# Relational sums of a graph layer: counts matrices replaced by gathered edge rows

## The chip, the cores and the metric

The kernel runs on one core of a Trainium2 chip, in one launch. The metric is the device time of the program in microseconds. The kernel before was timed three times: 2770.32 us in the median, 2766.78 to 2781.82. A profile was taken of one further execution, whose span from the first to the last instruction is 2772.8 us.

## The reference

There are 625 nodes with 1024 features and 10,625 edges, each with a source, a destination, a weight and one of 8 types. Two layers follow each other. Layer 0 has a graph convolution, linear attention and a mixture of 16 experts. Layer 1, cut to what matters:

```
xn  = layernorm(x)
u   = xn @ root + bias
for r in range(8):                         # the edge types, "relations"
    sums = segment_sum(xn[src] * (type == r), dst)     # 625 x 1024
    cnt  = segment_sum((type == r), dst)
    u    = u + (sums / max(cnt, 1)) @ weight[r]        # weight[r] is 1024 x 1024
z   = concat(u, xn) @ w_gate + b_gate
gnn = tanh(u) * z + xn * (1 - z)
mix = linear_attention(xn) @ Wout + bout               # 16 heads, needs Wqkv first
x   = x + gnn + mix
x   = x + small mixture of experts(layernorm(x))
```

All of it is in float32. The kernel gets float32 products out of TensorE's fp32r mode by splitting each operand into a high and a low part and adding three products (high by high, low by high, high by low).

## The kernel before

The 625 nodes are 5 blocks (T) of 125 (TP). The transposed normalized input lies in SBUF as T_h and T_l. A weight matrix of 1024 x 1024 comes in 8 chunks of 128 x 1024 (512 KB): SyncE loads chunk after chunk into three raw buffers (wr), ScalarE makes the high part (`a_high`, line 709), VectorE the low part (`v_low`, line 224), into two pairs ws0 and ws1. `t_nat` multiplies one half (512 columns) of such a matrix: 4 chunks, 10 steps each, 3 matmuls with 512 columns in every step, into 5 PSUM banks, one for each node block. 3 of the 8 banks are then free for other work.

Every engine runs one list of instructions in a fixed order. There is no planner. What is put between the steps of a product is written by slots: `blocks()` gives each chunk of 10 steps its first slot, and `t_nat(..., slot=)` calls `t_tally` after every step.

Layer 1 in the kernel before, in order:

1. `t_attention`: Wqkv products, feature maps, attention sums (24 chunks of Wqkv). ScalarE's table for exp is loaded once in it.
2. The window: root (8 chunks), Wout (8) and the product of relation 0 (8), 240 steps. Into them go 123 tallies. `t_tally` multiplies a one-hot of sources (blc, made by GpSimd, line 2220) with a step function of targets (bod, one ScalarE Sign activation of 128 x 628, line 2169), 2 matmuls of 314 columns in bf16. VectorE adds the two halves into an int16 accumulator (acc, line 220), and SyncE stores it to DRAM. Their differences along the nodes are, for each relation, the 625 x 625 matrix of edge counts (A).
3. `t_relations`: for each relation the product y_r = xn @ weight[r] (80 steps, 240 matmuls), ScalarE and VectorE take it out of PSUM as high and low parts (nat_h, nat_l), `t_count_in` sums the counts of each node (25 matmuls of 8 columns), and `t_sums` multiplies the counts matrix with y_r: 2 halves, 5 x 5 blocks, 2 parts, so 100 matmuls of 512 columns. VectorE scales them by 1/count and adds them to u (ua, line 220).
4. `t_gate`: xn and u times w_gate, 160 steps. u is transposed during the first 40 of them (line 2794); tanh, the difference with the kept xn (xnk) and the gate sums follow.

Ahead of that, in layer 0, the edges are sorted twice on VectorE and scattered to DRAM by GpSimd: by blocks of sources for the convolution, and into 40 buckets (8 relations by 5 blocks) for the tallies (`v_sort`). The convolution itself already works by one-hots: 96 pieces of 128 edges in 32 groups of 3, a group belonging to one node block.

Of the kernel before, what the change touches and what calls it, by code (L numbers as in the profile page):

```python
# [3 lines left out]
ALU = mybir.AluOpType  # L4
# [13 lines left out]
EC = 85  # L18
NCH, NBK = 123, 40
NG, GC = 32, 3  # L20
NW = NG * GC
TALLY0 = 18
# [217 lines left out]
class Program:  # L240
    def __init__(self, nc, a, out):
# [5 lines left out]
        self.d_edges = nc.dram_tensor("scr_edges", (128 * NCH, 4), F32).ap()  # L247
        self.d_adj = nc.dram_tensor("scr_adj", ((NBK + 1 + NCH) * 128, NT), I16).ap()
# [13 lines left out]
        self.tallied_at = {TALLY0 + 5 * c // 3: c for c in range(NCH)}  # L262
        self.regs = [nc.alloc_register(mybir.EngineType.DVE, f"adj{i}") for i in range(8)]
        self.slots = [nc.alloc_register(mybir.EngineType.SP, f"slot{i}") for i in range(4)]
# [3 lines left out]
    def memory(self, nc):  # L268
# [51 lines left out]
        pair("A", R3 + 15168, 3140)  # L320
# [12 lines left out]
        at("soh", U, NBK * EC, BF16)  # L333
        at("ssc", U + 6816, NBK * EC, BF16)
        at("st1", U + 13632, NBK // 2 * EC)

        for i in range(7):
            at(f"acc{i}", R3 + 20224 + i * 1280, NT, I16)
        for i in range(7):
            at(f"bod{i}", R3 + 30336 + i * 1280, NT, BF16)  # L340
        for i in range(4):
            at(f"blc{i}", R3 + 39296 + i * 256, 128, BF16)

        for i in range(2):
            at(f"steps{i}", R3 + i * 6304, T * NT, I16)
        at("brow_u", R1, 1024)
# [67 lines left out]
        small("oneb", 128, BF16)  # L414
        spair("om", 512)
        B = o[0]
        small("et1", 1280)
        at("seb", B, NCH * 4)
        at("bias", B + 1984, NCH)
        at("same", B + 2496, NCH + 1)  # L420
        at("brows", B + 3008, NCH, I32)
        at("bslot", B + 3520, NCH)
        at("bod7", B + 3520, NT, BF16)
        at("blc4", B + 4800, 128, BF16)
        at("row", B, 1024)
        at("rwp", B, 1024, F32R)
        at("none", B, NCH * 4)
# [3 lines left out]
        at("n32", B + 2880, NBK, I32)  # L431
        at("widx", B + 3040, EC, I32)
        at("dg", B + 3392, NCH + 1, F32R)
        at("idx", B + 4000, EC, I32)
# [4 lines left out]
        small("bkr", NCH + 1)  # L439
# [14 lines left out]
        small("shift", T)  # L454
        for n in ("lg", "pr", "o1", "o2", "q1"):
            small(n, T * 16)
# [25 lines left out]
    def weights(self):  # L482
# [54 lines left out]
        qkv = lambda c: W.add(("qkv", c), a["Wqkv"][c], 1024, 2, pool=c == 8)  # L537
# [11 lines left out]
        for r in range(8):  # L549
            for h in range(2):  # L550
                for i in range(4):
                    W.add(("rel", r, h, i), W2(a["rel"][r], 2 * i, 2 * i + 2, h), 1024, 2)
# [45 lines left out]
    def tensor(self, e):  # L598
        q = Line(e, self.counting)
        self.t_features(q)  # L600
        self.t_mix0(q)
        self.t_adjacency(q)
        self.t_spread(q)
        self.t_layernorm(q, 1)
        self.t_experts(q)
        self.t_layernorm(q, 2)
        self.t_attention(q)
        self.t_relations(q)
        self.t_gate(q)
        self.t_layernorm(q, 3)  # L610
        self.t_ffn(q)

    def scalar(self, e):
# [8 lines left out]
        self.a_high(q, ("qkv", 8))  # L622
        self.a_layernorm(q, 2)
        self.a_attention(q)
        self.a_relations(q)
# [4 lines left out]
    def vector(self, e):  # L630
# [8 lines left out]
        self.v_layernorm(q, 2)  # L639
        self.v_attention(q)  # L640
        self.v_relations(q)
# [4 lines left out]
    def gpsimd(self, e):  # L646
# [4 lines left out]
        self.p_low(q, ("qkv", 8))  # L651
        self.p_keep(q)
        self.p_tallies(q)
        self.p_relations(q)
        self.p_gate(q)

    def sync(self, e):
        q = Line(e, self.counting)
        a, m = self.a, self.m
        blocks = self.blocks()  # L660
# [6 lines left out]
        for c in self.W.all:  # L667
# [6 lines left out]
            n = self.W.of[c.key] - self.W.of["root", 0, 0] - 4  # L674
            if 0 <= n < 24:
                self.s_store_tallies(q, self.tallies(blocks[n][2]))
# [35 lines left out]
    def a_place(self, q, c):  # L712
# [5 lines left out]
        elif c.key == ("w1", 0):  # L718
            q.wait_ge(self.s("aggregated"), ("sum", 7, 1, T - 1))
# [37 lines left out]

    def t_first(self, q, key, L):

        outs = self.t_pair(q, key)  # L760
        hi, lo = self.t_chunk(q, key)
        for i, t in ((0, 2), (1, T - 1)):
            q.wait_ge(*self.ps.done(("ln", L, t), 1, "low"))
            for k in range(KD):
                c = slice(k * 128, (k + 1) * 128)
                ins = mm3(q.e, outs[i:i + 1], (hi[:, c], lo[:, c]), self.Tk(k)[i:i + 1], k == 0, k == KD - 1)
        ins.then_inc(*self.s("product").up(key))
# [24 lines left out]
    def t_nat(self, q, name, h, nk, lhs, ready=None, more=(), slot=None, last=None):  # L792
# [8 lines left out]
        for i in range((nk + 1) // 2):  # L801
# [6 lines left out]
            for at, (j, t) in enumerate(steps):  # L808
                k = 2 * i + j
                if ready:  # L810
                    q.wait_ge(*ready(k))
# [9 lines left out]
                if slot is not None:  # L821
                    self.t_tally(q, slot + 10 * i + at)
# [68 lines left out]

    def t_chunk_ends(self, q):
        e, m, ps = q.e, self.m, self.ps
        b, = ps.take("chunks", 1)
        for emptied in ps.before("chunks"):
            q.wait_ge(*emptied)
        q.wait_ge(self.landed("cst_all"), 0)
        q.wait_ge(self.s("sorted"), "chunk ends")
        mm(e, ps.one(b, 128, 0, NCH + 1), m["ones"][0:NCH, :], m["dg"][0:NCH, :], True, True).then_inc(*self.s("sort_sums").up("chunks"))
# [38 lines left out]
    def v_features(self, q):  # L938
# [32 lines left out]
        end, base = self.v_ends(q, "weighted", T, 1, 128 * GC, "wssc")  # L971
# [13 lines left out]
        off, at = m["off"][0:1, :], m["o2"][0:1, 0:NG]  # L985
        ts(e, at, self.iota[0:1, 0:NG], end[0:1, 0:1], None, ALU.is_ge).then_inc(*S.up())
        for b in range(1, T - 1):
# [2074 lines left out]
```

## Time and profile before

| | us |
|---|---|
| median of 3 runs | 2770.32 |
| profiled execution, span | 2772.8 |
| PE (matmul) busy | 2662.3, 96% |
| PEld (weight load) busy | 2167.4, 78% |
| DVE busy | 1726.8, 62% |
| ACT busy | 1289.3, 46% |
| POOL busy | 530.7, 19% |
| DMA mean | 165 GB/s, 458.31 MB |

PE is TensorE, PEld its weight loads, DVE VectorE, ACT ScalarE, POOL GpSimd, SP SyncE. Matmuls are pipelined and overlap in the record, so PE's busy share says that it always had something under way, and its rate is to be read from the starts of matmuls that follow each other. The profiled execution's own device time is not shown beside its span; the span lies 2.5 us above the median of the three runs.

### The profile page before, as it was taken

To read this page: it belongs to the slowest core of one execution; us is meant where nothing else is said; L and a number is where in the kernel's file an instruction comes from. 1 tells how busy PE (TensorE), PEld (TensorE's weight loads), DVE (VectorE), ACT (ScalarE), POOL (GpSimd) and SP (SyncE) were. 2 spreads that over 40 slices of the span, in tenths; PEclk is the share of its full clock that TensorE was granted. 3 is DMA by queue.
4 is the path that set the end of the run, shared out by engine and by line. 5 is a ranking of instruction groups with operands and counts; after the bars stand their busy time and mean duration, and the time that the engine had idled before them with its cause. 6 is when DMAs were issued, how large, how long until landed. Compare 5 with 4: busy or idle time off the path is not lost.

```text
span 2772.8 us, 35121 instructions
## 1 busy us (share of the span) xinstructions
PE 2662.3 (96%) x13835; PEld 2167.4 (78%) x13835; DVE 1726.8 (62%) x2061; ACT 1289.3 (46%) x1667; POOL 530.7 (19%) x502
## 2 busy tenths in 40 slices
PE   7999999999999999999989998999999999999999
PEld 6978788777777767666889997666788888878788
DVE  7579556788777887888655656886333233335353
ACT  4337225666667666777356656664111112212121
POOL 5869025223210000000200001443200000002100
PEclk9999999999999999999999999999999999999999
DMA  5342057999999999999621111555211122121212
GB/s 165 82 128 64 31 158 254 330 328 330 329 320 333 323 328 335 338 336 334 201 76 47 39 42 52 159 158 163 92 65 65 53 73 72 61 83 46 84 58 76
DMA packets 163198, 458.31 MB, mean 165 GB/s; under 512 B 26233, under 2 KB 54777, under 8 KB 163034
## 3 DMA queue, kind: packets, MB, share of 16 engines
q1 hardware_dynamic: 128122, 409.11, 42.4%
q0 software_dynamic: 20416, 33.77, 4.8%
q10 hardware_dynamic: 14496, 13.17, 1.5%
q8 instruction: 111, 1.82, 0.3%
q14 instruction: 53, 0.43, 0.1%
HBM read 412.13 MB, written 43.65 MB: 164 GB/s over the span
## 4 chain that ended last, share of the span: by engine, by line
PE 78%; DVE 9%; DMA 7%; ACT 3%; issue 2%; POOL 1%; SPq 0%; DVEq 0%; ACTq 0%; POOLq 0%
PE ps L199 77%; DMA er<-in_wd 3%; DVE es_l L224 2%; ACT es_h L709 2%; DMA er<-in_wg 1%; DVE od L216 1%; DVE Aw L212 1%; DMA scr_ei<-xn,sdi 1%; DMA wk<-in_Wk 1%; PE ps L1906 1%; DMA yg<-scr_eo,sgi 0%; POOL scr_ei L2099 0%; DVE T_l L224 0%; DVE x L212 0%; DVE ws_l L224 0%
## 5 line engine op out<-in xcount | busy, mean ns | idle before, releaser
L224 DVE TENSOR_TENSOR es_l<-er,es_h 128x1408 fp32r<-128x1408 f32 (+1 forms) x455 | 653.7, 1445 | 185.2 <-ACT es_h L709 181.8
L709 ACT ACTIVATE es_h<-er 128x1408 fp32r<-128x1408 f32 (+1 forms) x455 | 563.4, 1242 | 250.4 <-PE ps L199 166.4
L709 ACT ACTIVATE ws_h<-wr 128x1024 fp32r<-128x1024 f32 (+1 forms) x169 | 178.0, 1055 | 644.3 <-PE ps L199 635.1
L224 DVE TENSOR_TENSOR ws_l<-wr,ws_h 128x1024 fp32r<-128x1024 f32 x167 | 207.2, 1241 | 327.5 <-ACT ws_h L709 327.2
L199 PE MATMUL ps<-ws_h,T_h 128*125 128x512 f32 x880 | 355.9, 404 | 0.0
L199 PE MATMUL ps<-ws_l,T_h 128*125 128x512 f32 x880 | 347.4, 395 | 0.0
L199 PE MATMUL ps<-ws_h,T_l 128*125 128x512 f32 x880 | 347.3, 395 | 0.0
L199 PE MATMUL ps<-es_h,xe_h 128*98 128x512 f32 (+1 forms) x768 | 208.0, 379 | 11.5 <-DVE es_l L224 11.3
L199 PE MATMUL ps<-es_h,xe_l 128*98 128x512 f32 (+1 forms) x768 | 204.6, 374 | 0.0
L199 PE MATMUL ps<-es_l,xe_h 128*98 128x512 f32 (+1 forms) x768 | 204.6, 374 | 0.0
L199 PEld LDWEIGHTS ps<-ws_h,T_l 128*125 128x125 f32 x880 | 163.2, 185 | 41.7
L199 PEld LDWEIGHTS ps<-ws_h,T_h 128*125 128x125 f32 x880 | 163.5, 186 | 40.7 <-DVE ws_l L224 0.3
L199 PEld LDWEIGHTS ps<-ws_l,T_h 128*125 128x125 f32 x880 | 163.0, 185 | 37.6
L199 PEld LDWEIGHTS ps<-es_h,xe_h 128*98 128x98 f32 x768 | 119.2, 163 | 59.1 <-DVE es_l L224 19.9
L199 PEld LDWEIGHTS ps<-es_l,xe_h 128*98 128x98 f32 x768 | 125.0, 163 | 38.1
L199 PEld LDWEIGHTS ps<-es_h,xe_l 128*98 128x98 f32 x768 | 125.0, 163 | 38.1
L199 PE MATMUL ps<-T_h,ws_h 128*128 128x314 f32 x656 | 152.1, 309 | 1.0 <-DVE ws_l L224 0.7
L199 PE MATMUL ps<-T_l,ws_h 128*128 128x314 f32 x656 | 150.1, 307 | 0.0
L199 PE MATMUL ps<-T_h,ws_l 128*128 128x314 f32 x640 | 145.9, 307 | 0.0
L220 DVE SCALAR_TENSOR_TENSOR acc<-acc,same,ps 128x314 int16<-128x314 int16 x244 | 120.8, 537 | 35.3 <-PE ps L199 30.9
L220 DVE SCALAR_TENSOR_TENSOR ua<-ps,m,ua 125x512 f32<-125x512 f32 x80 | 60.0, 751 | 120.9 <-PE ps L199 120.9
L2169 ACT ACTIVATE bod<-cst,bias 128x628 bf16<-128x628 f32 x123 | 100.1, 818 | 70.9 <-PE ps L199 69.4
(455 smaller groups left out, 5271.4 us busy)
## 6 DMA issues: line engine op xcount, KB each, us to landing
er<-in_wg SPq DMA_DIRECT2D x128, 704.0 KB, 6.6
er<-in_wu SPq DMA_DIRECT2D x128, 704.0 KB, 5.9
er<-in_wd SPq DMA_DIRECT2D x176, 512.0 KB, 5.1
wr<-in_rel SPq DMA_DIRECT2D x64, 512.0 KB, 3.6
scr_adj<-acc SPq DMA_DIRECT2D x123, 157.0 KB, 2.4
wr<-in_Wqkv SPq DMA_DIRECT2D x24, 512.0 KB, 3.5
wr<-in_gate SPq DMA_DIRECT2D x16, 512.0 KB, 3.6
wr<-in_w SPq DMA_DIRECT2D x13, 512.0 KB, 3.6
```

The source lines that it names most:

```text
L199: return e.matmul(out, l, r, start=start, stop=stop, skip_group_check=True)
L212: return e.tensor_tensor(out, x, y, op)
L216: return e.tensor_scalar(out, x, s1, s2, op0) if op1 is None else e.tensor_scalar(out, x, s1, s2, op0, op1)
L220: return e.scalar_tensor_tensor(out=out, in0=x, scalar=s, in1=y, op0=op0, op1=op1)
L224: return e.tensor_tensor(lo, src, hi.bitcast(F32), ALU.subtract)
L709: q.e.activation(c.hi, c.at, ACT.Copy).then_inc(*self.s("high").up(c.key))
L1906: ins = q.e.transpose(ps.one(bs[f // 4], 128, (f % 4) * C0, C0), self.m["eh"][0:C0, f * 128:(f + 1) * 128], self.ident[0:C0, 0:C0])
L2169: q.e.activation(self.m[f"bod{c % 8}"], self.iota, ACT.Sign, bias=self.m["bias"][:, c:c + 1]).then_inc(*self.s("chunk_signs").up(c))
```

## The change

The edges are now sorted into 5 buckets by the block of the destination, in pieces of 128 edges, three pieces to a group, 96 pieces in 32 groups. `t_relations` moves ahead of `t_attention`. It makes y_r for all 8 relations, ScalarE alone takes them out of PSUM in float32, and SyncE stores them to DRAM (scr_y, 5000 rows of 4 KB). Once, after relation 1, `t_counts` makes edge counts by node and relation with 96 matmuls of 8 columns; VectorE turns them into 1/count, and GpSimd gathers for each edge its weight (96 indirect DMAs of 128 rows of 32 bytes).

The window is now root, Wout and the first four chunks of the gate (200 steps, of which slots 14 to 178 carry 96 sums). For each piece GpSimd gathers 128 rows of scr_y (512 KB, buffers gr0 to gr5), ScalarE makes the one-hot of destinations by two activations (Abs, then Relu) and the weighted high part, VectorE the weighted low part, and TensorE multiplies the one-hot with both, 4 matmuls of 512 columns. VectorE adds the two halves of each group into ua, which starts as the bias and not as the root product. The tallies, the counts matrices and the per-relation sums are gone.

The core of the diff:

```diff
+NR, NH, NS = 6, 3, 6
+SUM0, SUM1 = 14, 178
@@
+        self.summed_at = {SUM0 + c * (SUM1 - SUM0) // NW: c for c in range(NW)}
@@
+        self.t_relations(q)
         self.t_attention(q)
-        self.t_relations(q)
+        self.t_window(q)
         self.t_gate(q)
@@
+    def t_sum(self, q, slot):
+        c = self.summed_at[slot]
+        g, j = c // GC, c % GC
+        key = ("sum", g)
+        if j == 0:
+            ps.next = self.sum_next
+            ps.take(key, 2)
+            self.sum_next = ps.next
+        q.wait_ge(self.s("row_targets"), c)
+        q.wait_ge(self.s("rows_low"), c)
+        for h in range(2):
...
+            for i, part in enumerate((m[f"gh{c % NH}"], m[f"gl{c % NR}"])):
+                ins = mm(q.e, ps.one(ps.group[key][h], TP), m[f"gs{c % NS}"][:, 0:TP], part[:, h * 512:(h + 1) * 512],
+                         j == 0 and i == 0, j == GC - 1 and i == 1)
+            ins.then_inc(*self.s("summed").up((c, h)))
+    def a_rows(self, q, c):
+        off, to = m[f"go{c % 2}"], m[f"gs{c % NS}"]
+        if c >= NS:
+            q.wait_ge(self.s("summed"), (c - NS, 1))
+        else:
+            q.wait_ge(self.s("out_low"), 7)
+        q.e.activation(off, self.iota[:, 0:128], ACT.Abs, bias=m["gtl"][:, c:c + 1]).then_inc(*self.s("row_offsets").up(c))
+        q.wait_ge(self.s("row_offsets"), c)
+        q.wait_ge(self.s("row_weights"), 1)
+        q.e.activation(to, off, ACT.Relu, bias=m["sd"][:, 0:1], scale=-1.0).then_inc(*self.s("row_targets").up(c))
+        q.wait_ge(self.landed(f"rows{c % NR}"), c)
+        if c < NH:
+            q.wait_ge(self.s("attention_sums"), ("out", 7, 1))
+        else:
+            q.wait_ge(self.s("summed"), (c - NH, 1))
+        q.e.activation(m[f"gh{c % NH}"], m[f"gr{c % NR}"], ACT.Copy, scale=m["gw"][:, c:c + 1]).then_inc(*self.s("rows_high").up(c))
+    def v_rows(self, q, c):
+        stt(q.e, m[f"gl{c % NR}"], m[f"gr{c % NR}"], m["gw"][:, c:c + 1], m[f"gh{c % NH}"].bitcast(F32), ALU.mult, ALU.subtract).then_inc(*self.s("rows_low").up(c))
+    def v_sum(self, q, g):
+        for h in range(2):
...
+            tt(q.e, u, ps.one(ps.group["sum", g][h], TP), u, ALU.add).then_inc(*ps.out(("sum", g), h))
+    def p_rows(self, q):
...
+        q.wait_ge(self.s("attention_sums"), ("out", 7, 0))
+        for c in range(NW):
+            if c >= NR:
+                q.wait_ge(self.s("summed"), (c - NR, 1))
+            elif c > 1:
+                q.wait_ge(self.s("out_low"), 7)
+            of = bass.IndirectOffsetOnAxis(ap=m["gidx"][:, c:c + 1].bitcast(U32), axis=0)
+            e.indirect_dma_start(m[f"gr{c % NR}"], None, self.d_y[:, :], of).then_inc(*self.landed(f"rows{c % NR}").up(c))
@@ the transposes of u, inside the first four gate chunks
-                        if not h and part and t == T - 1 and 1 <= k <= T:
-                            self.t_turn_u(q, k - 1)
+                        if not h and part:
+                            self.t_sum(q, 160 + 10 * i + at)
+                            if t == T - 1 and 3 <= k:
+                                self.t_turn_u(q, k - 3)
```

ScalarE and VectorE prepare two pieces ahead of TensorE (`a_window`, `v_window`: `ahead = 2`); NR = 6 gather buffers, NH = 3 high parts, NS = 6 one-hots. xn and the bias bout are added to x by GpSimd at the start of `p_relations`, the kept xn (xnk) is loaded after the last gather is issued.

## Rows read from the trace of the kernel before

**Rows 1.** The page: busy time, share of the span and instructions of each engine.

```profile
PE 2662.3 (96%) x13835; PEld 2167.4 (78%) x13835; DVE 1726.8 (62%) x2061; ACT 1289.3 (46%) x1667; POOL 530.7 (19%) x502
```

**Rows 2.** Windows: start:end, us, busy by engine (instructions), PE clock, DMA share, GB/s.

```profile
1397.80:1709.80 312.00, 295.55 (x2089) 289.86 (x2090) 176.52 (x163) 188.88 (x322) 1.35 (x3) 0.99 0.13 46
1709.80:1930.10 220.30, 207.90 (x969) 142.18 (x968) 173.99 (x312) 131.05 (x164) 89.17 (x133) 1.00 0.50 151
1930.10:2532.00 601.90, 601.89 (x2683) 484.12 (x2682) 207.47 (x237) 101.24 (x128) 40.93 (x38) 0.99 0.22 70
```

**Rows 3.** Timeline of PE, end of a product, counts, sums: start us, us, instruction, count.

```profile
2009.62 0.40 PE L199 MATMUL ps<-ws_l,T_h 128*125 128x512 f32 x1
...
2013.33 0.39 PE L199 MATMUL ps<-ws_h,T_l 128*125 128x512 f32 x1
2013.56 2.88 PE L199 MATMUL ps<-ones,A_l 125*125 125x8 f32 x25
2016.30 0.77 PE L199 MATMUL ps<-nat_h,A_l 125*125 125x512 f32 x1
```

**Rows 4.** Groups by form, PE, 1690 to 2700: count, busy us, mean ns, idle before.

```profile
L199 PE MATMUL ps<-nat_h,A_l 125*125 125x512 f32 x200 | 80.3, 401 | 0.0
...
L199 PE MATMUL ps<-bod,blc 128*128 128x314 bf16 x246 | 53.9, 300 | 12.4 <-issue 11.1 <-DVE acc L2183 1.2
```

**Rows 5.** Timeline of PE, the two matmuls behind one tally in the window.

```profile
1804.73 0.50 PE L199 MATMUL ps<-ws_h,oh 128*125 128x512 f32 x1
1805.07 0.39 PE L199 MATMUL ps<-ws_l,oh 128*125 128x512 f32 x1
```

**Rows 6.** Timeline of PE, the first keys of the attention.

```profile
1425.71 0.55 PE L199 MATMUL ps<-om_h,zk_h 128*125 128x256 f32 x1 [3.30 <-ACT oT L2424]
```

**Rows 7.** Timeline of DVE, end of the attention.

```profile
1710.89 4.08 DVE L2498 RECIPROCAL rt<-rt 128x628 f32<-128x628 f32 x1
1715.01 0.81 DVE L212 TENSOR_TENSOR oT<-oT,rt 128x628 f32<-128x628 f32 x1
```

**Rows 8.** Groups by form, DVE, 1390 to 2700.

```profile
L224 DVE TENSOR_TENSOR ws_l<-wr,ws_h 128x1024 fp32r<-128x1024 f32 x123 | 154.6, 1257 | 280.9 <-ACT ws_h L709 280.9
...
L212 DVE TENSOR_TENSOR x<-ps,x 125x512 f32<-125x512 f32 x10 | 6.8, 683 | 0.0
...
L224 DVE TENSOR_TENSOR ol<-oT,oh 128x628 fp32r<-128x628 f32 x8 | 6.0, 806 | 2.9 <-ACT oh L2456 2.9
```

**Rows 9.** Tile yg: VectorE's use of the gathered rows, min/median/max ns.

```profile
L220 DVE SCALAR_TENSOR_TENSOR x<-yg,vs,x x10: 1279/1284/1285, 1350.8 to 1371.6; 125x1024 f32<-125x1024 f32 x10
```

**Rows 10.** Groups by form, ACT, 1390 to 2700.

```profile
L709 ACT ACTIVATE ws_h<-wr 128x1024 fp32r<-128x1024 f32 x122 | 129.3, 1061 | 549.7 <-PE ps L199 549.3
L2169 ACT ACTIVATE bod<-cst,bias 128x628 bf16<-128x628 f32 x123 | 100.1, 818 | 70.9 <-PE ps L199 69.4 <-DVE oT L212 1.5
...
L2433 ACT ACTIVATE va_h<-ps 125x128 fp32r<-125x128 f32 x8 | 2.8, 352 | 0.0
...
L2361 ACT ACT_TABLE_LOAD x1 | 1.3, 1283 | 0.0
```

**Rows 11.** Timeline of POOL, the first and the seventh of 10 gathers of 125 rows.

```profile
1340.97 1.27 POOL L2117 DMA_INDIRECT yg<-scr_eo,sgi  x1 [149.80 <-PE ps L199]
...
1350.90 2.26 POOL L2117 DMA_INDIRECT yg<-scr_eo,sgi  x1 [0.30 <-issue]
```

**Rows 12.** Tile yg: from issue to landing of those 10 gathers.

```profile
DMA to landing us min/median/max: 7.6/12.5/15.9
```

**Rows 13.** Line 2099: from issue to landing of 10 scatters of 125 rows.

```profile
DMA to landing us min/median/max: 8.5/11.7/18.7
```

**Rows 14.** Windows, columns as in Rows 2: gathers alone, then the experts' weights.

```profile
1349.00:1360.00 11.00, 11.00 (x78) 11.00 (x77) 7.32 (x7) 1.85 (x3) 8.15 (x5) 1.00 0.98 243
600.00:700.00 100.00, 99.04 (x470) 72.31 (x469) 83.56 (x73) 71.37 (x72) 29.12 (x22) 1.00 0.95 331
```

**Rows 15.** Timeline of DVE, one of two reduces of the sort into 40 buckets.

```profile
168.82 3.56 DVE L1056 TENSOR_REDUCE blk<-st 125x85 f32<-125x1700 f32 x1
```

More of the change, by code:

```diff
@@ L756, in t_pair @@
         return self.ps.halves(b)
[L758 to L767, printed above, removed]
     def t_trn(self, q, key, name="T"):
@@ L2135, in blocks @@
     def blocks(self):
-        keys = [(n, h, i) for n in (("root",), ("Wout",), ("rel", 0)) for h in range(2) for i in range(4)]
-        return [(b, (*n, h, i), 10 * b) for b, (n, h, i) in enumerate(keys)]
-    def tallies(self, first):
-        return [self.tallied_at[i] for i in range(first, first + 10) if i in self.tallied_at]
-    def tally_halves(self, c):
-        ps = self.ps
-        return [(i, slice(i * H, (i + 1) * H), ps.one(ps.group["tally", c][i], 128, 0, H)) for i in range(2)]
@@ L2149, in t_tally @@
-    def t_tally(self, q, slot):
+        keys = [(n, h, i) for n in ("root", "Wout") for h in range(2) for i in range(4)] + [("zgate", 0, 1, i) for i in range(4)]
+        return [(b, key, 10 * b) for b, key in enumerate(keys)]
+    def t_sum(self, q, slot):
         m, ps = self.m, self.ps
-        if slot not in self.tallied_at:
+        if slot not in self.summed_at:
             return
-        c = self.tallied_at[slot]
-        bs = ps.take(("tally", c), 2)
-        for emptied in ps.before(("tally", c)):
-            q.wait_ge(*emptied)
-        q.wait_ge(self.s("chunk_sources"), c)
-        q.wait_ge(self.s("chunk_signs"), c)
-        for h in range(2):
-            ins = mm(q.e, ps.one(bs[h], 128, 0, H), m[f"blc{c % 5}"], m[f"bod{c % 8}"][:, h * H:(h + 1) * H], True, True)
-        ins.then_inc(*self.s("tallied").up(c))
@@ L2570, in t_sums @@
-    def t_sums(self, q, r, h):
-        ps = self.ps
-        for t in range(T):
-            key = ("sum", r, h, t)
-            b, = ps.take(key, 1)
-            for emptied in ps.before(key):
-                q.wait_ge(*emptied)
-            for s in range(T):
-                q.wait_ge(*ps.done(("rel", r, h), s, "low"))
-                for j, part in enumerate(self.spread(h, s)):
-                    ins = mm(q.e, ps.one(b, TP), self.counts(r)[0:TP, s * NT + t * TP:s * NT + (t + 1) * TP], part,
-                             s == 0 and j == 0, s == T - 1 and j == 1)
-            ins.then_inc(*self.s("aggregated").up(key))
@@ L2730, in p_steps @@
-    def p_steps(self, q, r):
-        q.e.dma_start(rows(self.m[f"steps{r % 2}"], T), self.d_adj[r * T * 128:(r + 1) * T * 128, :].rearrange("(s p) n -> p s n", p=128)).then_inc(*self.landed(f"steps{r % 2}").up(r))
-    def all_stored(self, q):
-        for i in range(7):
-            q.wait_ge(self.landed(f"tally{i}"), NCH - 1 - (NCH - 1 - i) % 7)
+        q.wait_ge(*self.ud)
+        tt(q.e, u, self.ps.one(self.ps.group["root", h][t], TP), u, ALU.add).then_inc(*self.ps.out(("root", h), t))
+        self.ud = self.ps.done(("root", h), t)
@@ L2744, in t_gate @@
             group = ("z", h)
+            if not h:
+                ps.held, ps.next = set(range(8)) - set(self.slot_banks), self.slot_banks[0]
             bs = ps.take(group, T)
```

632 lines of the change are left out of this document (305 added, 327 removed).

## The prediction

> **What bounds the kernel now.** I read the page's busy times first, then windows by stage, then PE's timeline for the spacing of its matmuls. PE has something under way in 96% of the span [rows 1]. In a pure stretch of products 16 intervals of 512-column matmuls take 2013.33 - 2009.62 = 3.71 us, 0.232 us each [rows 3]. A relation's product is 240 of them, 55.7 us, and nothing else fits between. From 1397.8 us on there are three stages [rows 2]: attention 312.0 us, the window of root, Wout and relation 0 with the tallies 220.3 us, and seven products with eight sets of sums 601.9 us. In the last one PE is busy 601.89 of 601.90 us while VectorE has 207 us, ScalarE 101 us and the DMAs 22%. So the order of TensorE's instructions sets the time, and what counts is first how many matmuls go and come, then what makes TensorE wait.
>
> **What goes.** Sums and counts: 601.9 - 7 x 240 x 0.232 (389.8) = 212.1 us. They are the 800 matmuls of which [rows 4] shows one group of 200, eight times 25 count matmuls (2.74 us a set, 2013.56 to 2016.30 [rows 3]), and some us at the lower clock behind a set, where matmuls start 0.5 us apart. Tallies: 220.3 - 720 x 0.232 (167.0) = 53.3 us for 123 pairs, 0.433 us each. A pair of 314 columns is 2 x 314/512 x 0.232 = 0.285 us, so an insertion costs 0.148 us beyond its matmuls; one sees it in the 0.34 us between the two matmuls behind a tally, where 0.232 is usual [rows 5].
>
> **What comes on TensorE.** 96 pieces x 4 matmuls x 0.232 = 89.1 us. 96 count matmuls of 8 columns at 2.74/25 = 0.11 us are 10.5 us; with 3 us for the clock falling behind them, as it did behind the sets before, 13.5. The root, Wout, gate, Wqkv and relation products are the same matmuls in another order. Net on TensorE: -212.1 - 53.3 + 89.1 + 13.5 = -162.8 us.
>
> **What TensorE will wait for in the new window.** Take the first root matmul as 0. The 176 steps before the last sum are 176 x 3 x 0.232 = 122.5 us, with 89.1 us of sums 211.6 us if nothing waits. One piece comes each 1.71 steps: 1.19 + 0.93 + 0.148 = 2.27 us, so insertion alone adds 14.2 us. Against that, the others per piece:
> - VectorE: low part of a gathered row 1.28 [rows 9], two adds from PSUM by three 0.46, a weight chunk's low part 1.257 each 5.85 pieces 0.21, the 20 root and Wout adds 0.14 [rows 8]: 2.09 us.
> - ScalarE: high part 1.06, or 1.15 if a pointer for the scale costs anything (between 0 and 0.2, the row nearest being the Sign with its bias, no slower a column); Abs and Relu of 128 columns at most 0.352 each [rows 10]; weights 0.18: about 2.0 us.
> - GpSimd: 1.27 to 2.26 for an indirect DMA and 0.30 between two; six issues took 9.93 us, 1.66 each [rows 11].
> - DMA: gathers alone ran at 243 GB/s with the engines 0.98 busy, weights at 331 GB/s with 0.95 [rows 14]. 524,288 bytes are 2.16 us by the first, 1.58 by the second; the weight chunks add 0.27. So 1.85 to 2.43 us.
> - The loop through 6 buffers: landing 7.6 us unloaded [rows 12], ScalarE 1.06, VectorE 1.28, TensorE 0.93, handing over 0.7: 11.6/6 = 1.93 us. With the median landing of 12.5 us it is 16.5/6 = 2.75, with the slowest scatter, 18.7 us [rows 13], 22.7/6 = 3.8. Those were bursts into an idle loop, 125 rows each; the loop here holds fewer at a time, so I keep near the low end.
>
> Four stations near 2.1 us in a fixed order don't run at the slowest one's pace; I take 2.35 us, between TensorE's 2.27 and the DMA's 2.43. The start is late too: the attention's last result is ready at 1715.82, 6.0 us behind the first root matmul [rows 7] (1709.8 by [rows 2]), then eight copies and low parts at 0.81 [rows 8] free the buffers at about 13.4, and pieces from the third on are gathered only then. It lands at 21, the last 93 x 2.35 = 218.6 later, and 3.3 us pass to its sum: 242.9, which is 31 us over 211.6.
>
> **Rules weighed.** ScalarE loaded its table once in this whole stretch, and the 123 Sign activations, exp, square, copy and tanh shared it [rows 10]. The Trainium skill (ScalarE: Activation LUTs, Table sets: the hidden batching unit) says that relu, copy, identity and abs are in every set. No run here shows Abs or Relu; by that rule nothing is added, without it rival 4 holds.
>
> **What costs nothing, and its cover.** In the relations stage: each relation stores 2.56 MB and loads 4.19 MB, 20 us at 331 GB/s under 55.7 us of products. SyncE puts a store ahead of a chunk that is needed 4 chunks (27.8 us) later, and waits there only for ScalarE's last copy out of PSUM, which the chunk's own buffer release follows anyway. ScalarE's copies take the place of the high parts; VectorE loses its low parts and gets the edge one-hots and counts, single runs up to 11 us, beside 14 us of prepared weights; that cover is thin, a few us if it breaks. The 96 small gathers of weights are 159 us of GpSimd under six products (334 us). The last store of y must land before the first attention features: 8 us beside two Wqkv products (13.6 us). GpSimd's adds to x move to where it is idle.
>
> **Small terms.** The sort into 5 buckets takes VectorE operations like the 3.56 us reduce [rows 15] out of layer 0, where TensorE barely waits: -2.5 (0 to -8). The 3.30 us wait at the first keys [rows 6] came right behind the layernorm; there the relations now stand: -3.3 at best, I take that. The gate: u is transposed two steps of k later and block 4 is due 5 steps after; VectorE does 3.6 us a block, and xnk is loaded behind the last gathers: +3 (0 to 8).
>
> **The sum.** -162.8 + 31 - 2.5 - 3.3 + 3 = -134.6 us. The span of the profiled execution is 2772.8 us; its own device time is not shown, and the median of the runs lies 2.5 us below that span, so I subtract from both alike: span 2638, median 2770.3 - 134.6 = 2636 us. Its own range, with a pace of 2.27 to 2.55 us and the small terms: 2620 to 2655.
>
> **Rivals.**
> 1. The gathers hide fully. Then the window loses only the late start, 7 us, and insertion is free: -162.8 + 7 - 2.8 = -158.6, 2612 us. For it: VectorE, ScalarE and GpSimd all stand below 2.27, and 331 GB/s would be enough. Against: 0.148 us per insertion was paid for the tallies. The Trainium skill (DMA: Bandwidth & Descriptors, Anatomy of one DMA) gives about 2.0 us plus bytes/436e3 for a DMA issued by GpSimd, so an estimate of 3.2 us for one gather and 1.2 us of moving, which would make this the case; the 7.6 us and 243 GB/s measured here speak against it.
> 2. The gathers set the pace through the six buffers: 2.75 us a piece with the median landing. 21 + 93 x 2.75 + 3.3 = 280, 68.5 us over: -162.8 + 68.5 - 2.8 = -97, 2673 us. For it: half of the trace's gathers took 12.5 us or more [rows 12]. Against: those were issued seven deep into one burst.
> 3. The same loop at the slowest landing: 3.8 us a piece ends at 378, 166 over, 2771 us, no change; it is the point where the whole gain is gone, each further us of landing costs 15.5.
> 4. Slower: ScalarE becomes the bound by switching tables between Abs, Relu and Copy. Two loads of 1.283 us [rows 10] a piece make 2.0 into 4.6 us: 13.4 + 96 x 4.6 = 455, 243 over, 2770.3 - 162.8 + 243 - 2.8 = 2848 us. It decides from 3.8 us a piece. Against: one load in the whole attention and window before.
>
> **Chances.** Forecast 0.50, rival 1 0.15, rival 2 0.25, rival 3 0.05, rival 4 0.03, something unseen 0.02. A measurement tells about 0.5%, 14 us, from no change. Faster by more than that: the first three, 0.90; within it 0.04 and slower 0.06, out of rivals 3 and 4 and the rest. The range for 8 in 10 goes from below rival 1 to past rival 2: 2605 to 2690.
>
> **What would show it.** PE: 384 matmuls with gs, none with A or bod, and the relations stage at 55.7 us a product. The window from the first root matmul to the last sum: 243 us (rival 1 219, rival 2 280, rival 3 378, rival 4 455). Idle before the sums: by VectorE's gl, behind it DMA in rival 2, ScalarE in rival 4 with table loads listed. Landing of the gathers: 7 to 9 us; at 12 rival 2 holds. DMA share in the window near 0.9 at 250 to 300 GB/s. The first sum is 7 us late. The forecast is wrong if the relations stage runs at another pace than 55.7 us a relation, or if attention gets longer than 312 us.

## The result, and the profile after

The changed kernel takes 2750.72 us in the median of 4 runs (2749.98 to 2758.24), the kernel before 2772.22 beside it: a ratio of 0.9925, 95% interval 0.9906 to 0.9945. It is faster by 0.75%, where 2636 us were forecast. So 115 us of the forecast gain did not come. The page's busy times after, beside [rows 1]:

```profile
PE 2537.0 (92%) x13068; PEld 2070.9 (75%) x13068; DVE 1653.5 (60%) x1806; ACT 1363.8 (49%) x1832; POOL 645.2 (23%) x548
```

PE is busy 125 us less than before, and it no longer covers the span: 92% in place of 96%. The windows by stage, after, for relations, attention, the new window and the rest (columns: length, then busy us and instructions of each engine, granted clock, DMA share, GB/s), which answer to [rows 2]:

```profile
1392.00:1973.00 581.00, 473.83 (x2021) 367.35 (x2020) 135.22 (x96) 113.46 (x144) 121.07 (x112) 0.88 0.31 93
1973.00:2285.00 312.00, 296.50 (x2088) 290.69 (x2088) 173.06 (x152) 189.50 (x322) 3.10 (x4) 0.99 0.17 57
2285.00:2525.00 240.00, 222.05 (x921) 169.93 (x921) 201.31 (x207) 194.09 (x314) 132.88 (x104) 0.99 0.78 259
2525.00:2756.00 231.00, 218.08 (x1154) 188.66 (x1152) 110.37 (x174) 56.03 (x71) 29.88 (x10) 0.98 0.23 74
```

Attention is 312 us as before [rows 2], and the window, which I thought the uncertain part, is 240 us where 243 were forecast. The relations stage is 581 us where 445.4 + 13.5 = 459 were forecast (eight products of 240 matmuls at 0.232 us, and the counts). The whole miss, 122 us, lies in the stage that was said to cost nothing beyond its products. It has two places. The first is right at its start. VectorE's timeline after (columns: start, duration, engine, line, operation, count, idle before):

```profile
1394.95 25.62 DVE L225 TENSOR_TENSOR ws_l<-wr,ws_h 128x1024 fp32r<-128x1024 f32 x2
1429.58 1.22 DVE L225 TENSOR_TENSOR ws_l<-wr,ws_h 128x1024 fp32r<-128x1024 f32 x1 [9.01 <-ACT ws_h L722]
```

and GpSimd's there:

```profile
1395.23 11.64 POOL L213 TENSOR_TENSOR x<-x,lnx 125x1024 f32<-125x1024 f32 x5
1406.84 11.51 POOL L213 TENSOR_TENSOR x<-x,row 125x1024 f32<-125x1024 f32 x5
```

Two low parts of weight chunks take 25.6 us, where one takes 1.22. The first of the two alone has 24.5 us: its record begins 0.28 us ahead of GpSimd's first add to x and ends 1.1 us behind the tenth, and the ten adds, 2.3 us each, follow each other without a gap. What TensorE waited for in the same stretch:

```profile
PE ps L200 <- DVE ws_l L225: 19.8, 1, 19.8
```

The second place is 1586 to 1697 us. TensorE's matmuls in it:

```profile
1612.63 0.59 PE L200 MATMUL ps<-ws_h,T_h 128*125 128x512 f32 x1 [2.21 <-issue]
1615.43 0.59 PE L200 MATMUL ps<-ws_l,T_h 128*125 128x512 f32 x1 [2.21 <-issue]
1618.23 0.59 PE L200 MATMUL ps<-ws_h,T_l 128*125 128x512 f32 x1 [2.21 <-issue]
1621.03 0.59 PE L200 MATMUL ps<-ws_h,T_h 128*125 128x512 f32 x1 [2.21 <-issue]
```

They start 2.80 us apart in place of 0.232 [rows 3], and "issue" says that nothing the profile shows is waited for. The weight loads stand midway between them:

```profile
1614.03 0.28 PEld L200 LDWEIGHTS ps<-ws_l,T_h 128*125 128x125 f32 x1 [2.52 <-issue]
1616.83 0.28 PEld L200 LDWEIGHTS ps<-ws_h,T_l 128*125 128x125 f32 x1 [2.52 <-issue]
```

So it is every instruction of TensorE that comes 1.40 us behind the one before, weight load or matmul. ScalarE, whose copies wait for finished products, confirms the pace:

```profile
1630.90 1.06 ACT L722 ACTIVATE ws_h<-wr 128x1024 fp32r<-128x1024 f32 x1 [47.43 <-remote]
1647.64 0.60 ACT L2580 ACTIVATE y<-ps 125x512 f32<-125x512 f32 x1 [15.68 <-remote]
1664.44 0.60 ACT L2580 ACTIVATE y<-ps 125x512 f32<-125x512 f32 x1 [16.20 <-remote]
1681.24 0.60 ACT L2580 ACTIVATE y<-ps 125x512 f32<-125x512 f32 x1 [16.20 <-issue]
1693.14 0.60 ACT L2580 ACTIVATE y<-ps 125x512 f32<-125x512 f32 x1 [11.31 <-remote]
```

A node block's product ends every 16.80 us, six matmuls of 2.80. I call this the hole. GpSimd issues the 96 small gathers of weights in the same time, one each 1.28 us on average (name, count: shortest, median, longest ns, first and last start):

```profile
L2663 POOL DMA_INDIRECT wrow<-scr_inv,gdst x96: 943/946/1843, 1561.6 to 1683.2; - x96
```

They begin 25 us ahead of the hole, and it closes about 13 us behind the last. The windows after, first from the first gather to the end of the hole, then inside the hole alone:

```profile
1561.00:1699.00 138.00, 55.79 (x166) 34.70 (x164) 5.63 (x5) 10.25 (x14) 93.56 (x96) 0.61 0.22 35
1597.00:1683.00 86.00, 19.53 (x33) 9.12 (x33) 1.23 (x1) 2.85 (x4) 65.37 (x68) 0.50 0.19 22
```

The DMA engines are 0.19 busy in the mean, so their sum is not the limit. The granted clock in the hole is 0.50, the lower level of 1.2 GHz, but that is not the reason either: right behind the hole, still at that level, matmuls start 0.43 us apart (1697.03, 1697.45, 1697.88) and not 2.80.

### The profile page after: what moved, and what is told of

Read it like the earlier page. It is cut to its first block, busy times and chain, and to the rows that moved or that the text cites. A ratio compares the mean times of both kernels' runs of the same rounds, so it can differ in the third digit from the quotient of the medians.

```text
span 2756.3 us, 32941 instructions
## 1 busy us (share of the span) xinstructions
PE 2537.0 (92%) x13068; PEld 2070.9 (75%) x13068; DVE 1653.5 (60%) x1806; ACT 1363.8 (49%) x1832; POOL 645.2 (23%) x548
## 4 chain that ended last, share of the span: by engine, by line
PE 67%; DVE 13%; DMA 7%; issue 4%; ACT 4%; another core or an unknown queue 3%; POOL 1%; SPq 0%; DVEq 0%; ACTq 0%
PE ps L200 65%; DMA er<-in_wd 3%; DVE es_l L225 2%; DMA gr<-scr_y,gidx 2%; DVE ws_l L225 2%; ACT es_h L722 2%; DVE od L217 1%; DVE ua L213 1%; DVE Aw L213 1%; DMA er<-in_wg 1%; DVE gl L221 1%; DVE x L213 1%; ACT ws_h L722 1%; DMA scr_ei<-xn,sdi 1%
## 5 line engine op out<-in xcount | busy, mean ns | idle before, releaser
L225 DVE TENSOR_TENSOR ws_l<-wr,ws_h 128x1024 fp32r<-128x1024 f32 x167 | 229.6, 1376 | 557.2 <-ACT ws_h L722 492.8
L200 PE MATMUL ps<-ws_h,T_l 128*125 128x512 f32 x880 | 353.7, 402 | 32.0 <-issue 32.0
L200 PE MATMUL ps<-ws_l,T_h 128*125 128x512 f32 x880 | 353.2, 401 | 22.0 <-issue 22.0
L2095 POOL DMA_DIRECT2D xin<-scr_ei x16 | 9.4, 590 | 634.8 <-PE ps L1871 620.6
L2208 POOL DMA_INDIRECT gr<-scr_y,gidx x96 | 129.6, 1350 | 103.0 <-PE ps L200 81.2
```

The lines of the kernel that those rows point to most:

```text
L200: return e.matmul(out, l, r, start=start, stop=stop, skip_group_check=True)
L225: return e.tensor_tensor(lo, src, hi.bitcast(F32), ALU.subtract)
L2095: e.dma_start(m["xin"][0:C0, :], self.ei[x * C0:(x + 1) * C0, :]).then_inc(*self.landed("tokens").up(x))
L2208: e.indirect_dma_start(m[f"gr{c % NR}"], None, self.d_y[:, :], of).then_inc(*self.landed(f"rows{c % NR}").up(c))
```

## The experiments

Each is an edit of the changed kernel and timed beside the kernel before; ratios are to it, with 95% intervals. The code cuts are shortened; "..." stands for what is left out of a line or between lines.

**1. Without the small gathers.**

```
-        for c in range(NW):
-            e.indirect_dma_start(m["wrow"][:, c * 8:(c + 1) * 8], None, self.d_inv[:, :], of)...
+        e.memset(m["wrow"], 1.0)...
```

> Against the changed kernel this one leaves out the 96 indirect gathers of the inverse counts (the edge weights become 1 instead of 1 over the count). Theory A: the stream of 96 small gathers, one each 1.25 us, is what holds TensorE up from 1590 to 1703 us, where it ran 57 matmuls with no wait shown. Then the stretch shrinks from 113 us to what its matmuls take: the kernel loses 95 to 105 us, 2645 to 2656 us, and no stretch at half clock follows the counts. Rival B: TensorE is held up by something else at that place (the clock falling behind the 96 count matmuls, the stores of y, the fetching of its own instructions). Then the time stays at 2745 to 2755 us and the hole stays where it is.

Measured: 2650.05 us, ratio 0.956 (0.9539 to 0.958). The hole is gone; 100.7 us under the changed kernel. Theory A holds against B. (The edges are then weighed by 1 and not by 1 over the count.)

**2. The gathers three behind each chunk of products.**

```
+            if c % 3 == 0:      # g = c // 3: one chunk of relation 3, 4, 5 or 6 after the other
+                q.wait_ge(self.s("product"), ("rel", 3 + g // 8, g // 4 % 2, g % 4))...
             e.indirect_dma_start(m["wrow"]...
```

> The same 96 small gathers, but three behind each chunk of products from relation 3 on (7 us a chunk), so 2.3 us each on average in place of 1.25. Theory A1: it is the uninterrupted rate that holds TensorE up; then the hole goes as without the gathers, 2645 to 2660 us. Rival A2: each gather costs TensorE its share (100 us / 96 = 1 us), however they are spaced; then the time stays near 2750 us, with the loss spread over relations 3 to 6. Rival B (another cause at that place): the hole stays at 1590 us and the time at 2750 us.

Measured: 2653.57 us, 0.9573 (0.9553 to 0.9594), 3.5 us over experiment 1, whose four times overlap with these. All 96 gathers are there and cost that much at most: A2, a price of 1 us for each gather, falls.

**3. The adds to x spaced.**

```
+            q.wait_ge(self.s("product"), ("rel", 0, t // 3, t % 3))
             tt(e, x, x, m[f"lnx{t}"][0:TP, :], ALU.add)...
+            q.wait_ge(self.s("product"), ("rel", 1, t // 3, t % 3))
             tt(e, x, x, m["row"][0:TP, :], ALU.add)...
```

> GpSimd's ten adds to x each wait for a chunk of products of relation 0 or 1, in place of running back to back from 1397 us; the gathers stay as they are. Theory C: VectorE's low part of the second weight chunk (about 24 us instead of 1.26) is locked out by GpSimd's adds, which leaves TensorE idle for 19.8 us and at half clock for 20 us behind it. Then 22 to 32 us go: 2719 to 2729 us. Rival D: the 19.8 us come from the layernorm before or from the load of the chunk; then the gap stays and the time at 2745 to 2755 us.

Measured: 2627.41 us, 0.9483 (0.9464 to 0.9501). Both theories missed: this is 92 us under the lowest time that C allowed. The 20 us gap went, as C says, but the hole went with it, with the gathers untouched, and that nobody expected. VectorE's and GpSimd's timelines of this kernel:

```profile
1390.28 1.21 DVE L225 TENSOR_TENSOR ws_l<-wr,ws_h 128x1024 fp32r<-128x1024 f32 x1
1396.22 2.38 DVE L225 TENSOR_TENSOR ws_l<-wr,ws_h 128x1024 fp32r<-128x1024 f32 x1 [4.73 <-ACT ws_h L722]
```

```profile
1395.12 2.40 POOL L213 TENSOR_TENSOR x<-x,lnx 125x1024 f32<-125x1024 f32 x1 [4.58 <-PE ps L200]
```

One add delays one low part, from 1.21 to 2.38 us: it ends 1.1 us behind the add. That fits what the Trainium skill (SBUF — State Buffer, SBUF: two separate sides) says, that a GpSimd operation that reads SBUF and a VectorE operation with two SBUF inputs lock each other out of a shared port pair for a whole instruction; the trace agrees, with 1.2 us more for the low part. Ten adds in a row made one low part 24.5 us long: VectorE got no turn between them.

**4. Both.** The edits of 2 and 3.

> Both: paced small gathers and spaced adds. If theories A1 and C hold and their losses are separate, they add up: 2615 to 2635 us. If only one of them holds, the time is that one's (2650 or 2725 us).

Measured: 2628.45 us, 0.9483 (0.9466 to 0.95), inside what was expected, and no different from 3. Against experiment 2 the spaced adds are worth 25 us; the 19.8 us of wait and some 1.7 us at the lower clock behind it (eight steps of 0.45 us in place of 0.232, from 1419.5 to 1423.1 us) are seen in the trace of the changed kernel, the rest isn't placed. Experiment 4's windows by stage:

```profile
1387.00:1843.00 456.00, 451.39 (x2020) 359.60 (x2019) 123.78 (x95) 113.50 (x144) 137.43 (x112) 1.00 0.40 119
1843.00:2154.00 311.00, 295.56 (x2088) 289.84 (x2087) 173.01 (x152) 189.44 (x322) 3.10 (x4) 0.99 0.18 57
2154.00:2390.00 236.00, 220.83 (x919) 169.77 (x918) 201.33 (x207) 194.01 (x314) 133.09 (x104) 0.99 0.81 264
2390.00:2621.00 231.00, 218.05 (x1153) 188.71 (x1151) 110.25 (x174) 56.01 (x71) 29.87 (x10) 0.98 0.23 72
```

The relations stage is 456 us in place of 581. No other stage changed its length by more than 4 us.

Experiment 3 left a puzzle: full-rate gathers without a hole. Is it the adds that prepare it, or is it a matter of the moment?

**5. Gathers begun 7 us later or more, adds as they were.** One line ahead of the loop: `q.wait_ge(self.s("product"), ("rel", 3, 0, 0))`.

> The changed kernel as it is, with the 96 small gathers at their full rate (one each 1.25 us) but begun only behind the first chunk of relation 3, near 1600 us in place of 1561.6. Theory S (the gathers at this rate can stall TensorE, but it takes a meeting with something else at a certain moment, so that a shift decides): the hole of 108 us may go, 2650 us, or come elsewhere. Theory T (full-rate gathers stall TensorE whenever GpSimd's adds to x ran back to back before): the hole moves with the gathers, 2745 to 2755 us. Both leave the 20 us gap at 1399 us.

Measured: 2750.32 us, 0.9913 (0.9884 to 0.9941). As theory T says, the hole moves with the gathers: TensorE's wide steps go from 1639 to 1739 us. The gathers start at 1606.6 us, 208.5 us behind the stage's first matmul, where the changed kernel has 169.2. The shift is thus 39 us, near the 1600 us of the expectation; the 7 us of the run's name are wrong.

**6. Spaced adds, gathers 10 us later.** The edit of 3, and `q.wait_ge(self.s("product"), ("rel", 2, 1, 0))` ahead of the loop.

> The kernel with spaced adds, which had no hole and took 2627 us, with the full-rate gathers begun about 10 us later. Theory S: usually still none, 2622 to 2632 us, but a hole is possible (about 2725 us). Theory T: none, 2622 to 2632 us.

Measured: 2732.99 us, 0.9861 (0.9834 to 0.9887). The gathers start 158.2 us behind the stage's first matmul, where experiment 3 has 147.7. The hole is back with spaced adds: theory T falls, and of theory S, which gave the hole as the less likely case, only that it is possible holds. TensorE's waits from 1552 to 1693 us:

```profile
PE ps L200 <- issue: 78.0, 40, 6.1
```

**7. Spaced adds, gathers twice over.** The loop of 3 stands twice, the second behind the landing of the first.

> The kernel with spaced adds and the 96 small gathers run twice over at full rate, 240 us of them in place of 120. If each gather costs TensorE a little, the time rises by that; if they cost nothing while no hole opens, it stays at 2622 to 2632 us. Theory S gives a hole twice the time to open: then TensorE runs at 2.8 us a matmul in place of 0.232 until the last gather, 100 to 200 us more. Theory T: 2622 to 2632 us.

Measured: 2850.36 us, 1.0296 (1.0267 to 1.0324), 223 us over experiment 3, more than the 200 that theory S had at most: slower than the kernel before. The hole lasts as long as gathers are issued, over the 3.2 us between the two loops too, and 23 us longer. TensorE's waits:

```profile
PE ps L200 <- issue: 184.3, 87, 6.5
```

This run says something on experiment 3 too. The two kernels differ only behind the first 96 gathers, and yet here the hole opens inside those, 27 us behind the first gather. The first loop of each, as windows (here, from 1561 us, and in experiment 3 from end to end):

```profile
1561.00:1653.00 92.00, 23.82 (x40) 10.90 (x40) 1.23 (x1) 2.85 (x4) 69.91 (x73) 0.50 0.21 26
```

```profile
1535.00:1663.00 128.00, 128.00 (x551) 101.94 (x550) 22.11 (x18) 32.43 (x42) 98.59 (x96) 1.00 0.46 117
```

So it was not the spaced adds that kept the hole away in experiment 3. Counted from the stage's first matmul the gathers start at 146.1 us here and at 147.7 there; the 4 times of each kernel lie close together (2847 to 2859 and 2627 to 2631 us), but what tells the two apart isn't known.

**8. Gathers half a microsecond later.** `e.memset(m["wrow"][:, 0:256], 0.0)` ahead of the loop, adds as they were.

> The changed kernel with one GpSimd memset of 256 columns ahead of the 96 gathers, so that they begin some 0.3 to 0.6 us later and nothing else is changed. Theory S: so small a shift may already decide, 2650 us without the hole and 2750 us with it. Theory T: 2745 to 2755 us.

Measured: 2754.26 us, 0.9925 (0.9896 to 0.9953): the hole stays. The shift that was wanted did not come about: the gathers start 168.8 us behind the stage's first matmul, against 169.2 in the changed kernel, so this run repeats the changed kernel and says little on the moment.

Experiments 9, 10, 13, 14 and 15 start from experiment 6, which has the hole; 11 and 12 start from 4.

**9. A pause behind every fourth gather, waiting for nobody.**

```
+            if c and c % 4 == 0:
...
+                e.memset(m["ct"], 0.0)...
             e.indirect_dma_start(m["wrow"]...
```

> The kernel with spaced adds and gathers 10 us later, which had the hole (2733 us), with one GpSimd memset of 768 columns (0.74 us, about 1 us with what lies around it) behind every four small gathers, waiting for nobody outside GpSimd: about 1.5 us a gather in place of 1.25 to 1.28. The one run of full-rate gathers without a hole had 1.33 us a gather, because VectorE's low parts stopped GpSimd for 0.3 to 0.8 us once a chunk. Theory R (what decides is the rate of the small gathers, the limit lies between 1.29 and 1.33 us): no hole, 2622 to 2632 us. Rival F (the paced kernels have no hole because their gathers wait for TensorE, so that a slow TensorE slows them): an open loop has the hole still, 2720 to 2740 us.

Measured: 2626.1 us, 0.9484 (0.946 to 0.9508), no hole, with

```profile
L2671 POOL DMA_INDIRECT wrow<-scr_inv,gdst x96: 942/952/1879, 1546.1 to 1686.3; - x96
```

1.48 us a gather, and rival F falls: the gathers need not wait for TensorE, a pause of their own was enough here.

**10. Half the rows of each gather.** `gdst[0:64, ...]` and `wrow[0:64, ...]` in the loop.

> The same kernel with the hole (2733 us), and each of the 96 small gathers fetches 64 rows in place of 128 (the weights of the other rows are 1, so those edges are weighed wrongly). If the number of gathers (each with its 16 queue packets and its signals) holds TensorE up, the hole stays as long as the gathers run, 100 to 125 us: 2700 to 2740 us. If it is the number of rows, that is descriptors written a microsecond, the hole goes where a gather still takes about 0.95 us (half the rows in the same time), 2622 to 2632 us; it stays only if a gather of half the rows is also half as long.

Measured: 2627.34 us, 0.9497 (0.9471 to 0.9524), no hole, though

```profile
L2668 POOL DMA_INDIRECT wrow<-scr_inv,gdst x96: 899/903/1915, 1549.8 to 1675.8; - x96
```

one gather takes 903 ns against 946 and 96 are issued in 126 us against 122. The DMA queue shows about as many packets, 3040 against 3072 in experiment 6 (32 a gather and not the 16 of the expectation), which took 3.8% of the 16 engines' time against 11.7%. So the number of gathers, packets and signals did not bring the hole by itself, as far as one kernel can tell: experiment 3 shows that a kernel can be without it for a reason unknown.

**11. Short adds of the sums.** Experiment 4, and `v_sum` adds 8 columns in place of 512, so that most of the sum is left out.

> The kernel with both mended (2628 us), and VectorE adds only 8 of the 512 columns of each of the 64 sums to the aggregate (the output lacks the rest). VectorE's adds (0.69 us, 64 of them) then nearly vanish from the window: 2.09 us a piece become about 1.7. By my forecast, four stations close to 2.1 us a piece and 0.148 us for each insertion, TensorE's time is left mostly by the insertions and the late start: 5 to 10 us of the window's 31 us of waits go, 2618 to 2625 us. Rival: the waits are for the PSUM banks of the sums, which VectorE empties late; then 15 to 20 us go, 2608 to 2613 us. Second rival: the gathers' landing decides; then nothing goes.

Measured: 2621.23 us, 0.9463 (0.9429 to 0.9496). The interval overlaps that of 4, so the whole time does not tell. The window does: from the first root matmul (2159.94) to the last sum (2388.3) 228.4 us, against 2154.15 to 2389.6, 235.4, in experiment 4. 7 us, as the theory said; the rival wanted 15 to 20.

**12. First sum six steps later.** Experiment 4 with `SUM0, SUM1 = 20, 178`.

> The kernel with both mended (2628 us), the first sum 6 steps later (slot 20 in place of 14) and the last where it was. The forecast's late start costs 7 us, of which the trace shows 5.8 us ahead of the first sum; 6 steps are 4.2 us of products put in front of it. Theory: 3 to 6 us go, 2622 to 2625 us. Rival: the loop through the six buffers, not the start, sets the last sum's time; then the wait only moves behind, 2626 to 2631 us.

Measured: 2630.62 us, 0.95 (0.9478 to 0.9522), no gain. The rival holds: the wait for gl fell from 5.6 to 3.2 us, none of it longer than 1.2, and came back between the sums. TensorE's wait for VectorE's adds in the window, here and then in experiment 4:

```profile
PE ps L200 <- DVE ua L213: 14.0, 15, 2.1
```

```profile
PE ps L200 <- DVE ua L213: 9.1, 14, 1.3
```

**13. Plain DMAs in place of the gathers**, from experiment 6: `e.dma_start(m["wrow"][:, c * 8:(c + 1) * 8], self.d_inv[c:c + 128, :])`. The weights are then those of other rows.

> The kernel that had the hole (spaced adds, gathers begun 10 us later, 2733 us), with 96 plain DMAs of 128 rows of 32 bytes issued by GpSimd in place of the 96 indirect ones (the weights come from wrong rows). GpSimd's plain DMAs took about 0.55 us in the profile, so they come faster than 1.25 us. If rows written or moved a microsecond hold TensorE up, whoever makes them, the hole is there and shorter, 40 to 90 us of it: 2665 to 2715 us. If it is the indirection (the reading of indices), there is no hole: 2622 to 2632 us.

Measured: 2629.32 us, 0.9478 (0.9463 to 0.9494), no hole, with 96 DMAs of the same shape in 50 us:

```profile
L2665 POOL DMA_DIRECT2D wrow<-scr_inv x96: 535/537/581, 1557.7 to 1607.9; - x96
```

So 128 rows of 32 bytes at 2.4 times the rate did no harm when they were not indirect, for 50 us; the holes of the gathers opened 21 to 35 us behind the first.

**14. Gathers of other rows**, from experiment 6: `m["gidx"]` and `self.a["x"]` seen as rows of 8 values in place of `m["gdst"]` and `self.d_inv`.

> The kernel that had the hole (2733 us), and the 96 indirect gathers read 32-byte rows of x at the scattered indices of the sources in place of the neighbouring rows of the 20 KB table of inverse counts (the weights are wrong). If the reading of one small table in DRAM holds TensorE up, the hole goes: 2622 to 2632 us. If it is the issuing of the gathers, it stays: 2715 to 2745 us.

Measured: 2723.28 us, 0.9825 (0.9804 to 0.9846): the hole stays. Which table is read does not matter.

**15. A pause behind every eighth gather.** As 9, with `c % 8`.

> The kernel that had the hole (2733 us), with the memset of 0.74 us behind every eighth small gather, 1.36 to 1.42 us a gather in place of 1.28 (behind every fourth it was 1.48 us, without a hole). If the limit is on the mean rate and lies at 1.3 us, no hole: 2622 to 2632 us. If an unbroken run of more than some five gathers is enough to open it, the hole is there: 2700 to 2740 us.

Measured: 2719.47 us, 0.9811 (0.9794 to 0.9829), a hole, with

```profile
L2671 POOL DMA_INDIRECT wrow<-scr_inv,gdst x96: 942/950/1886, 1545.6 to 1674.1; - x96
```

1.35 us a gather, slower than the 1.33 of experiment 3 that had none. A limit on the mean rate, my reading until then, falls.

All runs with such a stream, by the mean distance of its DMAs:

| | us a gather | hole | us |
|---|---|---|---|
| 8; after; 5; 6; 14; 7 | 1.26 to 1.29 | yes | 2723 to 2850 |
| 3 | 1.33 | no | 2627.4 |
| 10 (64 rows) | 1.33 | no | 2627.3 |
| 15 (pause each eighth) | 1.35 | yes | 2719.5 |
| 9 (pause each fourth) | 1.48 | no | 2626.1 |
| 2 and 4 (three a chunk) | 2.30 | no | 2653.6 and 2628.5 |
| 13 (plain DMAs) | 0.53 | no | 2629.3 |

The mean is partly an effect of the hole and not its cause. Up to the 20th gather the distance was 1.34 us in the changed kernel and in 5, 6 and 14, 1.33 in 7, 1.27 in 8 and 1.39 in 15, and 1.36 in 3, which had no hole. Only then come the 1.25 us of the hole, in which VectorE has next to nothing to do and no longer holds up GpSimd.

## Why the prediction was wrong

**The step that failed** is "What costs nothing, and its cover", in two sentences. "The 96 small gathers of weights are 159 us of GpSimd under six products (334 us)" counted GpSimd's time and asked only whether it fits. It fits, in 123 us, and the stream holds up TensorE: 2750.7 - 2653.6 = 97 us (experiment 2, with 1 beside it and 6 and 7 from the other side). "GpSimd's adds to x move to where it is idle" looked at GpSimd and not at whom it locks out: 2653.6 - 2628.5 = 25 us (experiments 2 and 4), most of it 19.8 us of wait and the low clock behind it. Together that is 122 us, what the stage took too long. The kernel before had five of these adds back to back as well. They did no harm: beside them VectorE worked on sums out of PSUM, which kept their 0.75 us, and only the low part that met the last add got longer. Its timelines, GpSimd's and VectorE's:

```profile
1936.16 11.84 POOL L212 TENSOR_TENSOR x<-x,row 125x1024 f32<-125x1024 f32 x5 [7.17 <-DMA row<-in_brow]
```

```profile
1944.03 0.75 DVE L220 SCALAR_TENSOR_TENSOR ua<-ps,m,ua 125x512 f32<-125x512 f32 x1 [1.57 <-PE ps L199]
1946.33 0.75 DVE L220 SCALAR_TENSOR_TENSOR ua<-ps,m,ua 125x512 f32<-125x512 f32 x1 [1.55 <-PE ps L199]
1947.00 2.09 DVE L224 TENSOR_TENSOR ws_l<-wr,ws_h 128x1024 fp32r<-128x1024 f32 x1
```

These rows could have been read before the run: 2.09 us, where a low part takes 1.26, said what an add does to one, and the diff puts ten of them where TensorE needs the next low part. The condition that I gave for a wrong forecast, a relations stage at another pace than 55.7 us a relation, is the one that came.

**What goes, and what comes on TensorE.** Right. With both mended the kernel takes 2628.45 us, 8 under the forecast of 2636, and its relations stage is 456 us against 459. Inside that the counts were mis-sized, by tile:

```profile
L200 PE MATMUL ps<-ohr,csel x96: 166/166/180, 1525.9 to 1528.3; 128*128 128x8 bf16 x96
```

96 of them take 2.4 us, not 10.5. The 0.11 us each came from count matmuls on A_l, f32 in the row [rows 3]; these are bf16. In exchange the thin cover broke as feared: VectorE works on the counts without a gap from 1539 to 1554, 15 us where 11 were put at most, and the next low part is late (waits from 1520 to 1565):

```profile
PE ps L200 <- DVE ws_l L225: 4.6, 1, 4.6
```

**The window.** 239 us from the first root matmul (2285.55) to the last sum (2524.7) against 242.9: right in size. The stations, by line:

```profile
L221 DVE SCALAR_TENSOR_TENSOR gl<-gr,gw,gh 128x1024 fp32r<-128x1024 f32 x96 | 122.0, 1281 | 27.8 <-ACT gh L2170 27.8
L2170 ACT ACTIVATE gh<-gr,gw 128x1024 fp32r<-128x1024 f32 x96 | 110.0, 1146 | 30.7 <-PE ps L200 17.1 <-DMA gr<-scr_y,gidx 13.5
L2164 ACT ACTIVATE gs<-go,sd 128x128 fp32r<-128x128 f32 x96 | 38.7, 403 | 3.1
L2161 ACT ACTIVATE go<-cst,gtl 128x128 f32<-128x128 f32 x96 | 37.0, 386 | 0.7 <-DVE ol L225 0.7
```

1.28 and 1.15 us are as forecast, Abs and Relu 0.39 and 0.40 where I had 0.352 at most. What TensorE waited for, in the window:

```profile
PE ps L200 <- DVE ua L213: 12.1, 19, 1.4
PE ps L200 <- DVE gl L221: 5.5, 2, 5.4
```

The 5.4 us at the first sum are the late start (7 forecast). The rest of the waits is behind VectorE's adds out of the sums' PSUM banks, not behind gl as I had named it. The window stands 27.5 us over the 211.6 of its matmuls; 17.6 us are these waits, and the rest is 0.10 us for each piece put in, where 0.148 was forecast. Experiments 11 and 12 show that no single station decides: with both mended the window is 24 us over 211.6, of which shorter adds give 7 back and a later start none. Rivals 1, 2 and 3, with windows of 219, 280 and 378 us, are out. ScalarE waited for a gather 14 times, 13.5 us in all, and the DMAs stood at 0.78 and 259 GB/s, where about 0.9 and 250 to 300 were forecast; the trace gives no landing times for these gathers, so the forecast 7 to 9 us can't be judged. Rival 4 is out too; from 1973 to 2525 us ScalarE loads one table, the one of attention, as before [rows 10]. The Trainium skill (ScalarE: Activation LUTs, Table sets: the hidden batching unit) has abs and relu in every set, and by that the trace agrees.

**Small terms.** The wait at the first keys did not go with the layernorm: it stands there as before [rows 6], so -3.3 was wrong (TensorE's waits from 1985 to 2015):

```profile
PE ps L200 <- ACT oT L2430: 3.3, 1, 3.3
```

The gate and what follows come to 231.6 us behind the last sum, with the 16 steps of the gate that now stand ahead of it (11.1) 242.7, against 2772.8 - 2532.0 = 240.8 before [rows 2]: +2, forecast +3. The relations begin 5 us earlier; with the same code ahead that start lay between 1386 and 1400 us in other runs here, so the -2.5 of the sort can't be judged.

**What stays open.** Shown is that 96 indirect gathers of 128 rows in a close stream can bring TensorE to 2.80 us a matmul until they end, that it did not come with plain DMAs of that shape, with half the rows, with a pause behind every fourth or with three a chunk, and that the table does not matter. Not shown is what in TensorE is held up, and what opens the hole: 15 had it at 1.35 us a gather, 3 had none at 1.33, and 7 opened it where its instructions were still those of 3. So a single kernel without the hole, 9, 10 or 13, is weaker evidence than its time suggests; the paced gathers have two kernels, 2 and 4. In experiment 3 VectorE's low parts stopped GpSimd now and then (single gathers up to 1742 ns); once the hole is open VectorE has little to do and GpSimd runs unbroken, which would keep it open. That is argued only. One rival that experiment 1 named can be looked up: the loading of TensorE's own instructions. The queue that the profile calls "instruction" moves 16 KB about every 250 of TensorE's instructions, outside the hole and over it: at 1570.1 us, before the hole, in 0.88 us, and next at 1701.5 us, behind it, with 261 matmuls and weight loads between. So no such load was late or under way while each instruction took 1.40 us.

**A version that beats both** is experiment 4: 2628.45 us, 5.2% under the kernel before (0.9483, 0.9466 to 0.95), and 122 us under the change as made. Experiments 3 and 9 are as fast, but 3 has its gathers at the full rate, and no other kernel with that stayed free of the hole.

## What to carry to other kernels

An instruction moved to an idle engine is priced by whom that engine locks out and not by its own time: look at what stood between such instructions before, since a wait on a transfer may have been the pacing that kept a neighbour alive. Give a stream of small indirect gathers, and GpSimd operations on SBUF beside VectorE, a wait on the critical engine's progress for every few of them; here it cost some us at most and was worth 122. A run that is free of a stall for a reason you can't name is not a remedy: experiment 3 looked like one, and the next edits of it, 6 and 7, had the stall again. And when a stage is called free, its windows after are the first to read.

## What the runs showed of the hardware that I had not expected

- A stream of 96 indirect gathers of 128 x 32 bytes, 1.26 to 1.35 us each, slowed TensorE in seven kernels from 0.232 to 2.80 us a matmul, 1.40 us for each matmul or weight load, with no wait in the profile, and inside the hole the DMA engines 0.19 busy and 22 GB/s moved. It opened 21 to 35 us behind the first gather. The same shape as plain DMAs at 0.53 us each did nothing.
- GpSimd's adds back to back (ten of 2.3 us) made one VectorE instruction of 1.2 us last 24.5 us; one add alone cost it 1.2 us.
- A matmul of 8 columns in bf16 took 0.025 us from start to start.
